# Making the third weight piece of the one-hot rows on GpSimd in a graph network kernel (Trainium2)

## The chip, the cores and the metric

The kernel runs on one core of one Trainium2 chip. The metric is the device time of one execution in microseconds (us). A core has TensorE (PE, with its weight loads shown as PEld), VectorE (DVE), ScalarE (ACT), GpSimd (POOL) and SyncE (SP), each with an instruction queue of its own; the engines synchronise by semaphores. Tiles lie in on-chip memory (SBUF) or in the accumulator memory of TensorE (PSUM).

## The reference

Four graph layers run one after the other on 6250 nodes of 64 features and 206250 edges sorted by destination. Two of them end in a weighted sum over edges, and these two are what the change touches:

```
# second network: attention weights a = exp(e - max) / sum over the edges of a destination
out = segment_sum(a[:, None] * nfeat[src], dst, num_segments=6250)
# fourth network: given edge weights
messages = x[src] * edge_weights[:, None]
out = segment_sum(messages, tgt, num_segments=6250)
```

## The kernel before, in words

A weighted sum (`weighted_sum(n)`, n = 0 for the attention weights and n = 1 for the edge weights) does no gather of rows. The edges are held in blocks of 128 record slots by 64 positions, two blocks to a "pair", 37 pairs (`NDB`) to a sum. For each pair the kernel builds the matrix A[source node, slot] that holds the weight of each edge at its source, and then multiplies it with the node features X. A source node is written as two digits, a low one of 128 values (`P`) and a high one of 49 (`NB`). A is the product of two one-hot tables, built column by column on TensorE.

A pair takes 8 steps (`HS`) of 16 columns (`HC`), and a step takes 2 units of 8 columns (`UC`); so a pair is 16 units and each sum has 296 steps. The tables of a step lie in a ring of 2 (`ring = t % 2`).

- **VectorE, `onehots_of_step` (L1441 to L1461).** L1453 waits for the pair's codes and weights (`cw`), L1455 waits until TensorE has used up the ring's previous contents (`wgt_psum` of the step two earlier). Then three instructions: L1456 makes the high digit's one-hot rows `ohhi` (784 bf16 elements per partition) and signals `hi_made`; L1457 makes the low digit's rows `ohlo` (2048 elements) and signals `codes_ready`; L1461 multiplies `ohhi` by the weight. The float32 weight is split in three bf16 pieces, so that L1461 writes three tables, `ohw`, of 784 elements each (2352), and signals `hot_ready`. Every input and output of the three is in SBUF. In two of the eight steps of a pair VectorE also does small work: L1474 (two adds of a finished window into `acc`) and L1483 (two tables `spot`).
- **TensorE, `products_of_unit` (L932 to L961).** For n = 0 alone: L947, 16 matmuls of `ohlo` by `ohhi`, the adjacency counts. For both sums: it waits for `hot_ready` (L951, on even units) and for ScalarE (L953), then L959 does 48 matmuls, of 8 columns, 3 weight pieces and 2 halves. In 13 of a pair's 16 units (`MIXED`) `pair` (L963) adds L987: 4 of the 49 products X by A of the pair before, which are 8 matmul records in the profile. L995 and L977 fold and place the result once a pair. TensorE's program of a sum is not a hardware loop but is written out in full (L1002).
- **ScalarE, `pair` (L697).** L709 casts the adjacency of a unit to uint8 (n = 0 alone), L714 copies a unit of A from PSUM; each 128 x 784.
- **SyncE, `pair` (L513).** For n = 0 it stores the adjacency (L520). It waits for `hot_ready` of a pair's last step (L522) and loads the pair after next into `cw` (L525).
- **GpSimd (L574 to L636).** Index gathers and scatters by DMA in the earlier stages; its last gather (L615, reached through `gather_chunks`) is over before sum 0 begins. During both sums it runs nothing; between them it writes one row of ones (L636), after a wait for the end of sum 0.

All orders are written out by hand, with a semaphore behind each step.

Of the kernel before, what the change touches and what calls it, by code (L numbers as in the profile page):

```python
# [26 lines left out]
ALU = mybir.AluOpType  # L27
# [3 lines left out]
P = 128  # L31
# [3 lines left out]
NB = -(-N // P)  # L35
# [24 lines left out]
NDB = NRB // 2  # L60
UC = 8
GU = KC // UC
HC = 2 * UC
HS = P // HC
# [27 lines left out]
def gnn(nc, x_in, src, dst, etype, eweight, conv_W, conv_b, att_W, conv_nw, conv_nb, hid_W, hid_b, hid_nw, hid_nb,  # L92
        head_w, head_b, tail_w, tail_b, rel_w, W1_root, W1_rel, b1, W2_root, W2_rel, b2, out):
    with ExitStack() as ctx:
# [3 lines left out]
        def sem(name):  # L98
            return ctx.enter_context(nc.semaphore(name))
# [115 lines left out]
        cw = space[:, at:at + 5 * P].bitcast(BF16).rearrange("p (h x) -> p h x", h=2); at += 5 * P  # L215
# [94 lines left out]
        half_moved = sem("half_moved"); weight_rows = [sem(f"weight_rows{q}") for q in range(NWT)]; wt_psum = sem("wt_psum"); wt_split = sem("wt_split")  # L310
        wt_masked = sem("wt_masked"); denom_ready = sem("denom_ready"); denom_moved = sem("denom_moved"); denom_put = sem("denom_put")
        w_kept = sem("w_kept"); codes_stored = sem("codes_stored"); w_stored = sem("w_stored"); w_split = sem("w_split"); w_first = sem("w_first"); w_rest = sem("w_rest"); cw_loaded = [sem("cw_loaded0"), sem("cw_loaded1")]
        hi_made = sem("hi_made"); codes_ready = sem("codes_ready"); hot_ready = sem("hot_ready")
        adj_psum = sem("adj_psum"); adj_made = sem("adj_made"); wgt_psum = sem("wgt_psum"); wgt_made = sem("wgt_made")
        mixed = sem("mixed"); rowt_ready = sem("rowt_ready"); slot_rows = sem("slot_rows"); slots_copied = sem("slots_copied")
        spot_ready = sem("spot_ready"); spotted = sem("spotted"); summed = sem("summed"); half_summed = sem("half_summed")
# [18 lines left out]
        def _(sp):  # L335
# [177 lines left out]
            def pair(n, i, h, more=True):  # L513

                if n == 0:
                    for b in range(2):
                        sp.wait_ge(adj_made, i * (4 * GU) + (2 * h + b + 1) * GU)
                        sp.sem_inc(sp_ok, 1)
                        at = slice(4 * i + 2 * h + b, 4 * i + 2 * h + b + 1) if isinstance(i, int) else bass.ds(i * 4 + (2 * h + b), 1)
                        sp.dma_start(adj_d[at].rearrange("b p x -> (b p) x"), adj[:, b, :, :].rearrange("p a s -> p (a s)")).then_inc(adj_stored[b], 16)  # L520
                if more:
                    sp.wait_ge(hot_ready, i * (2 * HS) + (n * NDB * HS + (h + 1) * HS))  # L522
                    sp.sem_inc(sp_ok, 1)
                    at = slice(2 * i + h + 2, 2 * i + h + 3) if isinstance(i, int) else bass.ds(i * 2 + (h + 2), 1)
                    sp.dma_start(cw[:, h, :], cw_d[n, at].rearrange("d p x -> (d p) x")).then_inc(cw_loaded[h], 16)  # L525
# [48 lines left out]
        def _(pool):  # L574
# [37 lines left out]
            def gather_chunks(out, table, each):  # L612

                for b in range(NRB):
                    nc.gpsimd.indirect_dma_start(out=out[:, b * each:(b + 1) * each], out_offset=None, in_=table,  # L615
                                                 in_offset=bass.IndirectOffsetOnAxis(ap=half_rec[:, b:b + 1], axis=0)).then_inc(
                                                     rec_rows if table is rec_d else weight_rows[b // 8], 16)
# [12 lines left out]
            pool.wait_ge(wt_psum, NWT)  # L630
            pool.wait_ge(scan_stored, 16 * (LAYERS + 1))
            gather_chunks(wrow, scans_d.rearrange("(c e) a -> c (e a)", e=KC), KC)
            for h in range(2):
                pool.wait_ge(adj_stored[h], 16 * NDB)
            pool.wait_ge(summed, NDB)
            nc.gpsimd.memset(xT[F:F + 1, :], 1.0).then_inc(ones_back, 1)  # L636


        @block.scalar
# [132 lines left out]
        def _(pe):  # L772
# [159 lines left out]
            def products_of_unit(n, i, h, k):  # L932

                u = i * (4 * GU) + (n * NDB * 2 * GU + h * 2 * GU + k + 1)
                hot = i * (2 * HS) + (n * NDB * HS + h * HS + k // 2 + 1)
                early = k if isinstance(i, int) and n + i + h == 0 else 2
                ring = (k // 2) % 2
                if n == 0:
                    if k % 2 == 0:
                        pe.wait_ge(codes_ready, hot)  # L940
                    if early >= 1:
                        pe.wait_ge(adj_made, u - 1)
                    for c in range(UC):
                        col = (k % 2) * UC + c
                        for w in range(2):
                            lo, hi = KC * w, KC * w + KC
                            mm = nc.tensor.matmul(psum[:, w, c * NB:(c + 1) * NB], ohlo[lo:hi, ring, col // 2, :, col % 2],  # L947
                                                  ohhi[lo:hi, ring, col // 2, :, col % 2], start=True, stop=True)
                    mm.then_inc(adj_psum, 1)
                if k % 2 == 0:  # L950
                    pe.wait_ge(hot_ready, hot)  # L951
                if early >= 2:
                    pe.wait_ge(wgt_made, u - 2)  # L953
                for c in range(UC):
                    col = (k % 2) * UC + c
                    for r in range(3):
                        for w in range(2):
                            lo, hi = KC * w, KC * w + KC
                            mm = nc.tensor.matmul(psum[:, 2 + 2 * (k % 2) + w, c * NB:(c + 1) * NB], ohlo[lo:hi, ring, col // 2, :, col % 2],  # L959
                                                  ohw[lo:hi, ring, r, col // 2, :, col % 2], start=(r == 0), stop=(r == 2))  # L960
                mm.then_inc(wgt_psum, 1)  # L961
# [104 lines left out]
        def _(dve):  # L1066
# [374 lines left out]
            def onehots_of_step(n, i, h, t):  # L1441

                done = i * (2 * HS) + (n * NDB * HS + h * HS + t)
                ring = t % 2

                def pairs_of(v, wide):
                    return v.rearrange("p (s e) -> p s e", e=2).unsqueeze(2).to_broadcast([P, UC, wide, 2])

                def table(wide):
                    return digits[:, 0:wide, :].unsqueeze(1).to_broadcast([P, UC, wide, 2])  # L1450

                if t == 0:
                    dve.wait_ge(cw_loaded[h], i * 16 + 16 * (n * (NDB // 2 + 1 - h) + 1))  # L1453
                if not (isinstance(i, int) and n + i + h == 0 and t < 2):
                    dve.wait_ge(wgt_psum, i * (4 * GU) + 2 * (n * NDB * HS + h * HS + t - 1))  # L1455
                nc.vector.tensor_tensor(ohhi[:, ring, :, :, :], pairs_of(cw[:, h, P + t * HC:P + (t + 1) * HC], NB), table(NB), ALU.is_equal).then_inc(hi_made, 1)  # L1456
                nc.vector.tensor_tensor(ohlo[:, ring, :, :, :], pairs_of(cw[:, h, t * HC:(t + 1) * HC], P), table(P), ALU.is_equal).then_inc(codes_ready, 1)  # L1457
                dve.wait_ge(hi_made, done + 1)
                three = cw[:, h, 2 * P + t * 3 * HC:2 * P + (t + 1) * 3 * HC].rearrange("p (k s e) -> p k s e", k=3, e=2).unsqueeze(3).to_broadcast([P, 3, UC, NB, 2])
                each = ohhi[:, ring, :, :, :].unsqueeze(1).to_broadcast([P, 3, UC, NB, 2])  # L1460
                nc.vector.tensor_tensor(ohw[:, ring, :, :, :, :], each, three, ALU.mult).then_inc(hot_ready, 1)  # L1461

            def pair(n, i, h, bases, unit=True, mix=True, put=True):

# [156 lines left out]
```

## Time and profile before

| | us |
|---|---|
| median of 3 runs | 5945.24 (5943.95 to 5957.6) |
| the profiled execution, its own time | 5958.42 |
| its span in the profile | 5956.6 |
| sum 0: first to last start of L1456 | 2673.8 to 3997.8 |
| sum 1: first to last start of L1456 | 4918.7 to 5901.1 |
| PE, DVE, ACT, POOL busy | 3969.0, 3499.9, 2094.0, 736.3 |

Times are us from the span's start. A row of grouped instructions reads: line, engine, operation, output<-input, shapes, count | busy us, mean ns of one | idle us of the engine before them and what ended it. "x8" in a row of the timeline means that neighbouring instructions were merged.

### The profile page before, as it was taken

The page shows a single profiled execution, that of the slowest core. Times are in us where ns is not written, and L with a number is a line of the kernel's source. Part 1 is how long each engine was busy: PE and PEld are TensorE (multiplying, and loading weights), DVE is VectorE, ACT ScalarE, POOL GpSimd, SP SyncE. Part 2 cuts the span into 40 slices and gives each one's busy share as a digit, 9 for nine tenths or more (in the row PEclk, how much of TensorE's full clock was granted, in tenths as well). Part 3 has the DMA queues.
Part 4 walks back from the last instruction along what each step waited for, and adds up shares of the span by engine and source line. Part 5 has one row for each costly group of instructions (what it writes and reads, how often), then busy time and mean ns, then how long its engine had stood idle before and what let it go on. Part 6 is the DMA issues. An engine that isn't in the chain of part 4 may idle for free.

```text
span 5956.6 us, 236270 instructions
## 1 busy us (share of the span) xinstructions
PE 3969.0 (67%) x108221; PEld 3202.8 (54%) x108221; DVE 3499.9 (59%) x4015; ACT 2094.0 (35%) x2443; POOL 736.3 (12%) x758
## 2 busy tenths in 40 slices
PE   0015514804724813818888888887999988999997
PEld 0005513803723812806666666666988976666665
DVE  4532711731571741847676666666535539999997
ACT  4100000011001010007676676664635624555453
POOL 0033263072133033040000000000000000000000
PEclk9996755955865955959999999998989978999998
DMA  6722400520420501511111111114525510000000
GB/s 173 235 64 68 123 17 8 165 63 4 141 74 1 172 6 32 169 49 52 52 57 51 52 58 51 52 49 135 178 100 168 178 65 10 10 11 11 10 11 16
DMA packets 229352, 437.54 MB, mean 73 GB/s; under 512 B 115490, under 2 KB 139940, under 8 KB 228628
## 3 DMA queue, kind: packets, MB, share of 16 engines
q1 hardware_dynamic: 204784, 416.14, 22.1%
q0 software_dynamic: 23904, 10.76, 0.9%
q8 instruction: 635, 10.40, 0.7%
q14 instruction: 29, 0.24, 0.0%
HBM read 317.98 MB, written 112.84 MB: 72 GB/s over the span
## 4 chain that ended last, share of the span: by engine, by line
PE 62%; issue 15%; DVE 12%; ACT 3%; DMA 2%; another core or an unknown queue 2%; POOL 2%; SPq 2%; DVEq 0%; ACTq 0%; POOLq 0%
PE psum L987 16%; PE psum L959 12%; PE psum L836 12%; PE psum L1017 10%; PE psum L947 3%; PE psum L867 2%; PE psum L823 2%; DMA space<-digit_rows 2%; ACT space L709 1%; DVE space L1461 1%; PE psum L869 1%; DVE space L1143 1%; PE psum L1026 1%; PE psum L816 1%
## 5 line engine op out<-in xcount | busy, mean ns | idle before, releaser
L714 ACT COPY space<-psum 128x784 f32<-128x784 f32 x1184 | 966.2, 816 | 631.1 <-PE psum L959 629.0
L959 PE MATMUL psum<-space 64*128 64x49 bf16 x56832 | 990.4, 185 | 181.5 <-issue 152.3
L959 PEld LDWEIGHTS psum<-space 64*128 64x128 bf16 x56832 | 855.7, 95 | 391.2 <-issue 282.9
L987 PE MATMUL psum<-space,X 128*64 128x256 f32 x7252 | 1041.1, 398 | 13.6 <-issue 11.1
L836 PE MATMUL psum<-table,space 128*128 128x56 bf16 x24300 | 701.9, 189 | 347.8 <-issue 333.8
L836 PEld LDWEIGHTS psum<-table,space 128*128 128x128 fp8e4 x24300 | 671.3, 96 | 378.2 <-issue 367.2
L1268 DVE TENSOR_REDUCE space<-psum 128x1512 f32 x300 | 520.0, 1733 | 531.0 <-remote 379.0
L1461 DVE TENSOR_TENSOR space<-space 128x2352 bf16<-128x2352 bf16 x592 | 815.0, 1377 | 0.0
L1457 DVE TENSOR_TENSOR space<-space,V 128x2048 bf16<-128x2048 bf16 x592 | 721.5, 1219 | 0.0
L1017 PE MATMUL psum<-space 128*128 128x192 bf16 x7252 | 628.4, 247 | 23.9 <-DVE space L1536 23.9
L709 ACT CAST space<-psum 128x784 uint8<-128x784 f32 x592 | 482.9, 816 | 400.7 <-PE psum L947 398.1
L1017 PEld LDWEIGHTS psum<-space 128*128 128x128 bf16 x7252 | 594.9, 98 | 49.7 <-issue 48.9
L1456 DVE TENSOR_TENSOR space<-space,V 128x784 bf16<-128x784 bf16 x592 | 335.3, 566 | 460.9 <-PE psum L959 443.5
L987 PEld LDWEIGHTS psum<-space,X 128*64 128x64 f32 x7252 | 467.9, 138 | 197.4 <-issue 36.7
L816 PE MATMUL psum<-ident,X 128*64 128x128 f32 x539 | 104.5, 356 | 646.6 <-DVE X L1236 296.3
L751 ACT CAST space<-space 128x3200 bf16<-128x3200 uint8 x148 | 422.9, 2858 | 258.8 <-PE psum L1017 252.7
L1536 DVE CAST space<-space 128x3072 bf16<-128x3072 uint8 x148 | 260.5, 1760 | 307.2 <-PE psum L1017 304.9
L816 PEld LDWEIGHTS psum<-ident,X 128*64 128x64 f32 x539 | 64.1, 139 | 687.0 <-issue 317.0
L680 ACT ACTIVATE space<-space 128x1620 f32<-128x1620 f32 x4 | 6.2, 1552 | 985.9 <-DVE space L1377 985.9
L601 POOL DMA_INDIRECT heads_d<-spread,heads_at x280 | 261.3, 933 | 596.6 <-DVE spread L1255 512.9
L947 PEld LDWEIGHTS psum<-space 64*128 64x128 bf16 x9472 | 173.0, 95 | 261.9 <-issue 238.9
L609 POOL DMA_INDIRECT gath<-scans_d,ends x196 | 206.6, 1054 | 749.0 <-DMA scans_d<-space 690.5
(277 smaller groups left out, 2785.8 us busy)
## 6 DMA issues: line engine op xcount, KB each, us to landing
space<-onehots SPq DMA_DIRECT2D x300, 432.0 KB
space<-adj_d SPq DMA_DIRECT2D x148, 784.0 KB, 4.3
adj_d<-space SPq DMA_DIRECT2D x74, 784.0 KB, 3.6
onehots<-space SPq DMA_DIRECT2D x60, 432.0 KB, 2.9
space<-digit_rows SPq DMA_DIRECT2D x60, 378.0 KB
space<-cw_d SPq DMA_DIRECT2D x74, 160.0 KB, 3.3
cw_d<-space SPq DMA_DIRECT2D x4, 1184.0 KB
heads_d<-spread,heads_at POOLq DMA_INDIRECT x280
```

Of the source, the lines that this page charges most:

```text
L709: nc.scalar.copy(adj[:, b, :, :].rearrange("p a (w s) -> p w a s", w=2)[:, :, :, c:c + UC], psum[:, 0:2, 0:UC * NB].rearrange("p w (s a) - ...
L714: nc.scalar.copy(A[:, h, :, b * P:(b + 1) * P].rearrange("p a (w s) -> p w a s", w=2)[:, :, :, c:c + UC], psum[:, 2 + 2 * (k % 2):4 + 2 * ...
L751: nc.scalar.copy(adjb[:, r % 2, 0:HALF], adj8[:, r % 2, 0:HALF]).then_inc(cast_act, 1)
L836: mm = nc.tensor.matmul(pb[(h % 2) * NBK + b][:, t * HI:(t + 1) * HI], ohr[:, h, c:c + P].bitcast(FP8), table[:, r, :], start=(r == 0), st ...
L947: mm = nc.tensor.matmul(psum[:, w, c * NB:(c + 1) * NB], ohlo[lo:hi, ring, col // 2, :, col % 2], ohhi[lo:hi, ring, col // 2, :, col % 2], ...
L959: mm = nc.tensor.matmul(psum[:, 2 + 2 * (k % 2) + w, c * NB:(c + 1) * NB], ohlo[lo:hi, ring, col // 2, :, col % 2], ohw[lo:hi, ring, r, co ...
L987: mm = nc.tensor.matmul(pb[6][half:half + F, 0:2 * P], X[:, a, :], A[:, 1 - h, a, :], start=(a < 2), stop=(a >= NB - 2))
L1017: mm = nc.tensor.matmul(pb[r % 2][:, 0:3 * F].rearrange("p (k f) -> p k f", k=3), adjb[:, r % 2, a * P:(a + 1) * P], pieces[:, :, a * F:(a ...
L1268: nc.vector.tensor_reduce(peF[:, bass.ds(t, CH)].rearrange("p (b t) -> p b t", t=PB), banks, AX, ALU.max).then_inc(pick_read, 1)
L1456: nc.vector.tensor_tensor(ohhi[:, ring, :, :, :], pairs_of(cw[:, h, P + t * HC:P + (t + 1) * HC], NB), table(NB), ALU.is_equal).then_inc(h ...
L1457: nc.vector.tensor_tensor(ohlo[:, ring, :, :, :], pairs_of(cw[:, h, t * HC:(t + 1) * HC], P), table(P), ALU.is_equal).then_inc(codes_ready, 1)
L1461: nc.vector.tensor_tensor(ohw[:, ring, :, :, :, :], each, three, ALU.mult).then_inc(hot_ready, 1)
```

## The change

The third of the three products of L1461 moves to GpSimd. VectorE's instruction covers pieces 0 and 1 (1568 elements), and a GpSimd multiply covers piece 2 (784 elements) and signals a new semaphore `third_ready`. GpSimd waits for `hi_made` of the step. TensorE (at L951) and SyncE (at L522) each wait for `third_ready` in addition to `hot_ready`. GpSimd runs the 296 steps of sum 0 behind its last gather and ahead of the wait for the end of sum 0, and the 296 steps of sum 1 behind the row of ones.

```diff
@@ SyncE, pair
                     sp.wait_ge(hot_ready, i * (2 * HS) + (n * NDB * HS + (h + 1) * HS))
+                    sp.wait_ge(third_ready, i * (2 * HS) + (n * NDB * HS + (h + 1) * HS))
                     sp.sem_inc(sp_ok, 1)
@@ GpSimd
             gather_chunks(wrow, scans_d.rearrange("(c e) a -> c (e a)", e=KC), KC)
+            def third_of_step(n, i, h, t):
+
+                ring = t % 2
+                pool.wait_ge(hi_made, i * (2 * HS) + (n * NDB * HS + h * HS + t + 1))
+                third = cw[:, h, 2 * P + t * 3 * HC + 2 * HC:2 * P + (t + 1) * 3 * HC].rearrange("p (s e) -> p s e", e=2).unsqueeze(2).to_broadcast([P, UC, NB, 2])
+                nc.gpsimd.tensor_tensor(ohw[:, ring, 2, :, :, :], ohhi[:, ring, :, :, :], third, ALU.mult).then_inc(third_ready, 1)
+
+            def thirds_of_weights(n):
+
+                for h in range(2):
+                    for t in range(HS):
+                        third_of_step(n, 0, h, t)
+                with pool.Fori(1, NDB // 2) as i:
+                    for h in range(2):
+                        for t in range(HS):
+                            third_of_step(n, i, h, t)
+                for t in range(HS):
+                    third_of_step(n, NDB // 2, 0, t)
+
+            thirds_of_weights(0)
             for h in range(2):
                 pool.wait_ge(adj_stored[h], 16 * NDB)
             pool.wait_ge(summed, NDB)
             nc.gpsimd.memset(xT[F:F + 1, :], 1.0).then_inc(ones_back, 1)
+            thirds_of_weights(1)
@@ TensorE, products_of_unit
                     pe.wait_ge(hot_ready, hot)
+                    pe.wait_ge(third_ready, hot)
@@ VectorE, onehots_of_step
-                three = cw[:, h, 2 * P + t * 3 * HC:2 * P + (t + 1) * 3 * HC].rearrange("p (k s e) -> p k s e", k=3, e=2).unsqueeze(3).to_broadcast([P, 3, UC, NB, 2])
-                each = ohhi[:, ring, :, :, :].unsqueeze(1).to_broadcast([P, 3, UC, NB, 2])
-                nc.vector.tensor_tensor(ohw[:, ring, :, :, :, :], each, three, ALU.mult).then_inc(hot_ready, 1)
+                two = cw[:, h, 2 * P + t * 3 * HC:2 * P + t * 3 * HC + 2 * HC].rearrange("p (k s e) -> p k s e", k=2, e=2).unsqueeze(3).to_broadcast([P, 2, UC, NB, 2])
+                each = ohhi[:, ring, :, :, :].unsqueeze(1).to_broadcast([P, 2, UC, NB, 2])
+                nc.vector.tensor_tensor(ohw[:, ring, 0:2, :, :, :], each, two, ALU.mult).then_inc(hot_ready, 1)
```

## Rows read from the trace of the kernel before

**Rows 1.** Busy time by stretch: most of sum 0, then most of sum 1.

```profile
core 0: us, PE busy (x) PEld busy (x) DVE busy (x) ACT busy (x) POOL busy (x), PEclk, DMA share, GB/s
2750.00:3987.00 1237.00, 1073.49 (x38786) 771.33 (x38786) 853.64 (x961) 864.78 (x1200) 0.00 (x0) 0.97 0.14 53
5000.00:5880.00 880.00, 848.48 (x28842) 597.94 (x28842) 813.88 (x925) 440.25 (x594) 0.00 (x0) 1.00 0.04 10
```

**Rows 2.** L1456 alone, sum 0 and then sum 1: first and last start.

```profile
L1456 DVE TENSOR_TENSOR space<-space,V x296: 559/568/570, 2673.8 to 3997.8; 128x784 bf16<-128x784 bf16 x148
...
  PE psum L959: 383.1, 291
```

```profile
L1456 DVE TENSOR_TENSOR space<-space,V x296: 556/567/570, 4918.7 to 5901.1; 128x784 bf16<-128x784 bf16 x148
...
  PE psum L959: 60.4, 124
```

**Rows 3.** The waits of sum 1 from 5000 to 5880: us in total, times, longest.

```profile
DVE space L1456 <- PE psum L959: 53.2, 113, 0.5
PEld psum L959 <- DVE space L1461: 25.7, 65, 0.6
PE psum L959 <- DVE space L1461: 17.2, 33, 0.5
```

**Rows 4.** Busy time of one whole pair of sum 1.

```profile
5303.46:5330.00 26.54, 25.63 (x876) 18.07 (x878) 24.66 (x28) 13.34 (x18) 0.00 (x0) 1.00 0.04 10
```

**Rows 5.** The page's groups: the three table instructions, both sums.

```profile
L1461 DVE TENSOR_TENSOR space<-space 128x2352 bf16<-128x2352 bf16 x592 | 815.0, 1377 | 0.0
L1457 DVE TENSOR_TENSOR space<-space,V 128x2048 bf16<-128x2048 bf16 x592 | 721.5, 1219 | 0.0
...
L1456 DVE TENSOR_TENSOR space<-space,V 128x784 bf16<-128x784 bf16 x592 | 335.3, 566 | 460.9 <-PE psum L959 443.5
```

**Rows 6.** Timeline of VectorE in sum 1, a step without a wait for TensorE.

```profile
5318.60 1.38 DVE L1461 TENSOR_TENSOR space<-space 128x2352 bf16<-128x2352 bf16 x1
5319.89 0.56 DVE L1456 TENSOR_TENSOR space<-space,V 128x784 bf16<-128x784 bf16 x1
5320.37 1.22 DVE L1457 TENSOR_TENSOR space<-space,V 128x2048 bf16<-128x2048 bf16 x1
5321.50 1.38 DVE L1461 TENSOR_TENSOR space<-space 128x2352 bf16<-128x2352 bf16 x1
```

**Rows 7.** Groups of VectorE in that pair of sum 1: the small work.

```profile
L1474 DVE TENSOR_TENSOR space<-psum,space 64x128 f32 x2 | 0.6, 279 | 0.1
L1483 DVE TENSOR_SCALAR V<-iota_row,slot_rel 128x128 f32<-128x128 f32 x2 | 0.5, 282 | 0.0
```

**Rows 8.** What GpSimd runs in the whole span, apart from other DMAs.

```profile
L636 POOL MEMSET space<- 1x6288 f32 x1 | 5.3, 5334 | 1374.0 <-DVE space L1474 1374.0
L575 POOL IOTA iota_row<- 128x128 f32 x1 | 0.2, 228 | 0.4 <-POOLq L1611 0.4
...
L577 POOL IOTA iota_col<- 128x1 f32 x1 | 0.1, 127 | 0.0
L1611 POOL MEMSET const-bfloat16-1.0<- 128x1 bf16 x1 | 0.1, 106 | 0.0
```

**Rows 9.** Timeline of GpSimd: the gap between two of its instructions.

```profile
2301.36 0.95 POOL L601 DMA_INDIRECT heads_d<-spread,heads_at  x1 [0.30 <-issue]
```

**Rows 10.** Busy time where sum 1 starts, with no L987 in it yet.

```profile
4934.00:4943.00 9.00, 6.83 (x312) 6.42 (x307) 9.00 (x10) 4.88 (x6) 0.00 (x0) 0.50 0.02 4
```

**Rows 11.** Timeline of TensorE: at the lower clock, then at full clock.

```profile
4939.23 2.18 PE L959 MATMUL psum<-space 64*128 64x49 bf16 x96 [0.72 <-DVE space L1461]
```

```profile
3323.11 1.97 PE L987 MATMUL psum<-space,X 128*64 128x256 f32 x8
...
3325.01 0.52 PE L947 MATMUL psum<-space 64*128 64x49 bf16 x16
```

```profile
5303.34 1.08 PE L987 MATMUL psum<-space,X 128*64 128x256 f32 x8
```

More of the change, by code:

```diff
@@ L312, in gnn @@
         w_kept = sem("w_kept"); codes_stored = sem("codes_stored"); w_stored = sem("w_stored"); w_split = sem("w_split"); w_first = sem("w_first"); w_rest = sem("w_rest"); cw_loaded = [sem("cw_loaded0"), sem("cw_loaded1")]
-        hi_made = sem("hi_made"); codes_ready = sem("codes_ready"); hot_ready = sem("hot_ready")
+        hi_made = sem("hi_made"); third_ready = sem("third_ready"); codes_ready = sem("codes_ready"); hot_ready = sem("hot_ready")
         adj_psum = sem("adj_psum"); adj_made = sem("adj_made"); wgt_psum = sem("wgt_psum"); wgt_made = sem("wgt_made")
```

## The prediction

> **What bounds the kernel now.** I began with the busy shares by stretch. In most of sum 0 [rows 1] TensorE is busy 1073.49 of 1237 us (87%), VectorE 853.64 (69%) and ScalarE 864.78 (70%); in most of sum 1 TensorE is busy 848.48 of 880 (96%) and VectorE 813.88 (92%). GpSimd does nothing in either. So in sum 0 TensorE leads and VectorE waits; in sum 1 the two run almost level.
>
> Next the pace. L1456 starts once a step; 295 intervals from first to last start [rows 2] give (3997.8 - 2673.8) / 295 = 4.49 us a step in sum 0, 35.9 us a pair, and (5901.1 - 4918.7) / 295 = 3.33 us a step in sum 1, 26.6 us a pair. Before L1456 VectorE idles for TensorE's L959 for 383.1 us in sum 0, but only 60.4 us in sum 1.
>
> Then the waits of sum 1 [rows 3]. They go both ways: VectorE waits 53.2 us for TensorE's L959, and TensorE waits 17.2 us (its weight loads 25.7) for VectorE's L1461. The pair of 26.54 us [rows 4] shows what is to be had at most: TensorE is busy 25.63 us of it, so taking VectorE away altogether gives 0.91 us a pair.
>
> **What leaves VectorE.** The three table instructions take 566, 1219 and 1377 ns for 784, 2048 and 2352 elements [rows 5]. From 2048 to 2352 that is 158 / 304 = 0.52 ns an element, and 784 elements less make L1461 1377 - 407 = 970 ns. The cost per element is the same line through all three shapes, so I expect no other rate for 1568 elements. Unblocked, a step of VectorE runs from one L1461 to the next in 5321.50 - 5318.60 = 2.90 us [rows 6]; it becomes 2.49. With the small work, 2 x 0.28 + 2 x 0.28 us, taken at 1.1 a pair [rows 7], VectorE needs 8 x 2.90 + 1.1 = 24.3 us a pair now and 21.0 afterwards, if nothing else touches it.
>
> **What GpSimd gets.** 296 multiplies in each sum, of 784 bf16 elements with two inputs. The trace has no GpSimd arithmetic at all. Nearest are a memset of 6288 elements in 5334 ns, 0.85 ns an element, and iotas with (228 - 127) / 127 = 0.80; a one-element memset is 106 ns [rows 8]. One pass at the memset's rate is 784 x 0.85 + 0.1 = 0.77 us: the lower bound. Two reads and a write, each a pass of its own, are 3 x 0.67 + 0.1 = 2.1 us: the upper bound. I take 1.8 us, because this instruction has all three streams where the memset has one, so it is nearer the upper end. Between GpSimd instructions 0.30 us pass [rows 9]; I keep 0.3 a step for handing over.
>
> The Trainium skill (GPSIMD Engine Reference, section 3.1) gives about 2.6 cycles of 1.2 GHz for an element of a two-input op, which would be an estimate of 1.7 us here; no row shows it, and the sum by it would be some 40 us lower.
>
> **Do the two run side by side?** That is what decides. Rows show nothing against it and nothing for it: there is no stretch in which GpSimd reads tiles while VectorE works. So both ends must be priced. If they overlap freely, 1.8 + 0.3 us of GpSimd fit in a step of 3.33 us, and its cost is nil (the cover is VectorE's own 1219 + 970 ns behind `hi_made`, about as long). If GpSimd and VectorE exclude each other while reading SBUF, the multiply is added to VectorE's time: a step is 2.49 + 1.8 + 0.3 = 4.6 us. VectorE has no instruction in a step that isn't a two-input read of SBUF, so GpSimd could hide only in VectorE's idle time. I take the second.
>
> The Trainium skill speaks for the second (SBUF — State Buffer, section "Who interferes with whom"): a VectorE instruction with two SBUF inputs and a GpSimd instruction that reads SBUF exclude each other, and whichever comes later stands still until the first has ended. No row shows this; by the rule the time is the serial one, without it that of the first rival.
>
> **The sum.** A pair takes VectorE and GpSimd together 8 x 4.6 + 1.1 = 37.9 us. Who wins a handover doesn't matter: if VectorE always goes first it runs at most two steps ahead (the ring), must then wait for TensorE, and GpSimd catches up in that wait. Sum 1: 37.9 - 26.6 = 11.3 us a pair, times 37 = +418 us. Sum 0: 37.9 - 35.9 = 2.0, times 37 = +74 us. In sum 0 TensorE is also idle 13% of its pair [rows 1], 4.8 us, much of it ended by nothing that a row names; when VectorE leads, such a pause is partly absorbed by the ring and partly added. I take half of it, 2.4 x 37 = +89 us. Together +581 us.
>
> **Edits at nothing.** TensorE's added wait costs its issue only; behind it are L959 and all else of TensorE, which is why a late third is a late step, counted above. SyncE's added wait delays L525 by one multiply at a pair's end, while these codes are due a pair later (26 us or more); the adjacency store queued behind it comes due four steps later. GpSimd's queue holds nothing else during the sums, its last gather ends before them, and the row of ones waits for the end of sum 0 anyway.
>
> The profiled execution took 5958.42 us, 13 above the median of 5945.24. The increments belong to one execution and are laid on the median: 5945 + 581 = 6526 us, **my forecast (chance 0.62)**. Its own range, from multiplies of 1.5 to 2.1 us and all or none of the pauses, is 6330 to 6730: 0.3 us a step is 8 x 0.3 x 74 = 178 us, and the pauses 89 up or down.
>
> **Rivals.**
> 1. *Free overlap, faster (0.12).* VectorE has 21.0 us of work a pair and TensorE 25.6, so TensorE leads throughout sum 1. It decides if a multiply beside VectorE's reads lengthens neither and stays below some 3 us. Gain: 0.91 x 37 = 34 us, and 8 x 0.41 = 3 us in the first pair, which has no L987 and follows VectorE [rows 10]; nothing in sum 0, where VectorE waits already. Time 5908. For it: the free cycles of GpSimd and the 17.2 us of waits in rows 3. Against: the gain's ceiling is low.
> 2. *Overlap that pays for itself (0.04).* The two-engine slowdown just fills VectorE's 3.3 us of a pair: 5930 to 5960.
> 3. *Short or partial exclusion (0.10).* With 0.77 us the step is 3.56 us and the pair 29.6: 3.0 x 37 = +111 in sum 1, none in sum 0, 6056. Up to 1.5 us, some 6330.
> 4. *TensorE's clock falls too (0.12).* Where sum 1 starts, with TensorE idle 0.72 us before each 96 matmuls [rows 11], the granted clock is 0.50, which is the 1.2 GHz level [rows 10]. In the new kernel TensorE would have 3.5 us of work in 4.6, gaps of about 1.1 us a step. At that level a unit's L959 takes 2.18 / 2 = 1.09 us, L987 1.97 us against 1.08, L947 0.52 us [rows 11]. A pair of sum 1 is then 16 x 1.09 + 12.25 x 1.97 + 2 = 43.6 us, above the 37.9 of VectorE, and one of sum 0 8.3 more, 51.9. All the time at it: (43.6 - 26.6 + 51.9 - 35.9) x 37 = 1221 us, 7166. But so paced TensorE has no gaps and the clock should return, so half of what lies above the serial sum: 6526 + 320 = 6846.
>
> That the change doesn't do what it says is the case where VectorE's two-piece instruction keeps its 1.38 us; with exclusion that adds 0.41 x 8 x 74 = 243 us. I see no reason for it.
>
> **Numbers.** Faster by over 0.3% 0.12; within 0.3% (about what a measurement of this kernel can tell from no change) 0.04; slower 0.84. The range runs from the short multiply's 6060 to 6900, just over the half of rival 4: it holds the forecast, nearly all of 3 and some 0.7 of 4, about 0.80.
>
> **What would show it.** Right: L1461's successor at 0.97 us alone; VectorE's or GpSimd's recorded durations stretched, or idle before VectorE's instructions that ends with GpSimd; L1456's pace near 4.6 us in sum 1; TensorE waiting for GpSimd or VectorE in most steps. Wrong: L1456 to L1461 unchanged in length beside a GpSimd multiply, and a pace of 3.2 us in sum 1. A granted clock under 0.9 in the sums speaks for rival 4; a multiply recorded at 0.8 us for rival 3.

## The result, and the profile after

The changed kernel takes 6167.85 us (median of 4 runs, 6163.02 to 6175.68) against 5944.59 us (4 runs of the kernel before on the same chip): a ratio of 1.0373, 95% interval 1.0352 to 1.0394. It is slower, as forecast, but by 223 us and not by the 581 of the forecast. The profiled execution has a span of 6170.8 us (before: 5956.6). Below, a table instruction is named by its line in the changed kernel: L1479, L1480 and L1484 on VectorE are the former L1456, L1457 and L1461, L982 and L1010 on TensorE the former L959 and L987; L639 is GpSimd's multiply.

The page's groups, which answer to [rows 5]:

```profile
L639 POOL TENSOR_TENSOR space<-space 128x784 bf16<-128x784 bf16 x592 | 1498.8, 2533 | 1953.2 <-DVE space L1479 1953.2
...
L1484 DVE TENSOR_TENSOR space<-space 128x1568 bf16<-128x1568 bf16 x592 | 1254.5, 2119 | 0.0
...
L1480 DVE TENSOR_TENSOR space<-space,V 128x2048 bf16<-128x2048 bf16 x592 | 719.0, 1214 | 0.0
...
L1479 DVE TENSOR_TENSOR space<-space,V 128x784 bf16<-128x784 bf16 x592 | 349.2, 590 | 264.6 <-PE psum L982 251.3
```

The instruction that lost a third of its elements went from 1377 to 2119 ns. Its mean hides two kinds; the line's own view gives them (duration min/median/max):

```profile
L1484 DVE TENSOR_TENSOR space<-space x592: 956/2267/2275, 2660.1 to 6109.4; 128x1568 bf16<-128x1568 bf16 x198
```

0.96 us is what 1568 elements cost (forecast: 0.97), 2.27 us is that and 1.31 us more. In the timeline, 289 of the 296 in sum 0 and 236 of the 296 in sum 1 are of the long kind.

Where the time went is seen from the pace of L1479, as in [rows 2]; here first sum 0, then sum 1:

```profile
L1479 DVE TENSOR_TENSOR space<-space,V x296: 550/567/569, 2658.5 to 3984.5; 128x784 bf16<-128x784 bf16 x148
...
  PE psum L982: 151.6, 134
...
L1479 DVE TENSOR_TENSOR space<-space,V x296: 546/553/1579, 4902.7 to 6107.8; 128x784 bf16<-128x784 bf16 x148
...
  PE psum L982: 99.8, 75
```

Sum 0 lasts 3984.5 - 2658.5 = 1326.0 us, before it was 1324.0: nothing. What VectorE lost came out of its wait for TensorE, which fell from 383.1 to 151.6 us. Sum 1 lasts 6107.8 - 4902.7 = 1205.1 us, before it was 982.4: +222.7, the whole loss. (The two profiled spans differ by 214.2 us: the stages ahead of sum 0 were 15 us shorter in this execution, and the end behind sum 1 is 7.5 us longer.) A pair takes 32.7 us there in place of 26.6.

The timeline of VectorE and GpSimd in sum 1 shows the usual pattern:

```profile
5515.22 0.55 DVE L1479 TENSOR_TENSOR space<-space,V 128x784 bf16<-128x784 bf16 x1
5515.69 1.21 DVE L1480 TENSOR_TENSOR space<-space,V 128x2048 bf16<-128x2048 bf16 x1
5515.85 2.41 POOL L639 TENSOR_TENSOR space<-space 128x784 bf16<-128x784 bf16 x1 [1.78 <-DVE space L1479]
5516.83 2.27 DVE L1484 TENSOR_TENSOR space<-space 128x1568 bf16<-128x1568 bf16 x1
5519.02 0.55 DVE L1479 TENSOR_TENSOR space<-space,V 128x784 bf16<-128x784 bf16 x1
```

A step is 5519.02 - 5515.22 = 3.80 us, which is the forecast's 2.49 and 1.31. There is no gap in it: the stretched instruction is where VectorE stands still. The multiply is recorded from 0.16 us after L1480's start for 2.41 us, 0.9 us longer than the 1.50 us that it takes when it gets its turn at once (18 of the 296 in sum 1). So up to L1480's end it stands still too.

In 60 steps of sum 1 L1484 is short: 42 multiplies are passed over. Such a multiply asks during L1480, doesn't get its turn when L1480 ends, and waits until VectorE stops for TensorE. For 24 of them that is right behind L1484 of the same step, after 0.9 us. For the other 18 VectorE first runs a second step, whose own multiply queues behind the overdue one:

```profile
5903.74 0.55 DVE L1479 TENSOR_TENSOR space<-space,V 128x784 bf16<-128x784 bf16 x1
5904.22 1.21 DVE L1480 TENSOR_TENSOR space<-space,V 128x2048 bf16<-128x2048 bf16 x1
...
5904.38 7.25 POOL L639 TENSOR_TENSOR space<-space 128x784 bf16<-128x784 bf16 x2 [1.78 <-DVE space L1479]
...
5905.36 0.96 DVE L1484 TENSOR_TENSOR space<-space 128x1568 bf16<-128x1568 bf16 x1
...
5906.24 0.55 DVE L1479 TENSOR_TENSOR space<-space,V 128x784 bf16<-128x784 bf16 x1
5906.72 1.21 DVE L1480 TENSOR_TENSOR space<-space,V 128x2048 bf16<-128x2048 bf16 x1
5907.85 0.96 DVE L1484 TENSOR_TENSOR space<-space 128x1568 bf16<-128x1568 bf16 x1
5910.24 1.08 PEld L982 LDWEIGHTS psum<-space 64*128 64x128 bf16 x48 [3.65 <-issue]
...
5913.65 0.57 DVE L1479 TENSOR_TENSOR space<-space,V 128x784 bf16<-128x784 bf16 x1 [4.84 <-PE psum L982]
```

VectorE runs two steps in full, at their unblocked lengths. Only when the ring stops it at 5908.8 do the two multiplies run. TensorE's weight loads meanwhile idle 3.65 us, its matmuls 3.2 (the view says "issue", but what it needs is the third piece), and VectorE then waits 4.84 us for TensorE. There are 18 such stalls on the 37 pairs of sum 1; 17 of them end in a wait of L1479 of 3.6 to 5.5 us, 73.8 us in all of the 99.8 for which VectorE idles before L1479.

Every one of the 42 multiplies belongs to the step right behind VectorE's small work of the pair, L1497 (24) or L1506 (18), where L1479 follows that work without a gap; no other step's multiply is the first to be passed over. Why a small instruction ahead of the step has this effect, no run here shows.

The granted clock is 0.88 in sum 1, where it was 1.00. Behind a stall it is 0.50, the 1.2 GHz level; the second row is the part of the 4.84 us in which TensorE works again:

```profile
5000.00:6000.00 1000.00, 868.53 (x26641) 605.59 (x26642) 914.17 (x855) 408.50 (x549) 640.58 (x245) 0.88 0.03 8
5910.24:5913.65 3.41, 3.38 (x110) 2.59 (x112) 0.00 (x0) 0.81 (x1) 1.39 (x1) 0.50 0.16 48
```

### The profile page after: what moved, and what is told of

Its sections match the earlier page's. It is cut to its first block, busy times and chain, and to the rows that moved or that the text cites. A ratio compares the mean times of both kernels' runs of the same rounds, so it can differ in the third digit from the quotient of the medians.

```text
span 6170.8 us, 237478 instructions
## 1 busy us (share of the span) xinstructions
PE 4071.7 (66%) x108221; PEld 3268.0 (53%) x108221; DVE 3936.5 (64%) x4015; ACT 2096.0 (34%) x2443; POOL 2239.6 (36%) x1350
## 4 chain that ended last, share of the span: by engine, by line
PE 53%; issue 18%; DVE 18%; POOL 3%; DMA 2%; another core or an unknown queue 2%; ACT 2%; SPq 1%; DVEq 1%; ACTq 0%; POOLq 0%
PE psum L1010 11%; PE psum L858 11%; PE psum L1040 10%; PE psum L982 9%; DVE space L1484 5%; PE psum L969 3%; PE psum L889 2%; POOL gath L610 2%; PE psum L845 2%; DMA space<-digit_rows 2%; DVE space L1479 2%; PE psum L891 1%; DVE space L1166 1%; DVE space L1480 1%
## 5 line engine op out<-in xcount | busy, mean ns | idle before, releaser
L639 POOL TENSOR_TENSOR space<-space 128x784 bf16<-128x784 bf16 x592 | 1498.8, 2533 | 1953.2 <-DVE space L1479 1953.2
L1484 DVE TENSOR_TENSOR space<-space 128x1568 bf16<-128x1568 bf16 x592 | 1254.5, 2119 | 0.0
L982 PE MATMUL psum<-space 64*128 64x49 bf16 x56832 | 1026.9, 188 | 321.8 <-issue 178.0
L982 PEld LDWEIGHTS psum<-space 64*128 64x128 bf16 x56832 | 894.6, 97 | 556.7 <-issue 328.2
L1010 PE MATMUL psum<-space,X 128*64 128x256 f32 x7252 | 1087.5, 413 | 12.8 <-issue 10.4
L1480 DVE TENSOR_TENSOR space<-space,V 128x2048 bf16<-128x2048 bf16 x592 | 719.0, 1214 | 0.0
L1010 PEld LDWEIGHTS psum<-space,X 128*64 128x64 f32 x7252 | 481.7, 143 | 208.5 <-issue 52.6
L1479 DVE TENSOR_TENSOR space<-space,V 128x784 bf16<-128x784 bf16 x592 | 349.2, 590 | 264.6 <-PE psum L982 251.3
```

What stands on the lines that cost most here:

```text
L639: nc.gpsimd.tensor_tensor(ohw[:, ring, 2, :, :, :], ohhi[:, ring, :, :, :], third, ALU.mult).then_inc(third_ready, 1)
L1010: mm = nc.tensor.matmul(pb[6][half:half + F, 0:2 * P], X[:, a, :], A[:, 1 - h, a, :], start=(a < 2), stop=(a >= NB - 2))
L1484: nc.vector.tensor_tensor(ohw[:, ring, 0:2, :, :, :], each, two, ALU.mult).then_inc(hot_ready, 1)
```

## The experiments

The theory: **exclusion**. While GpSimd reads SBUF, VectorE's instruction stands still, and the other way round. Rivals: **traffic** (any GpSimd instruction, or the added signals, slow VectorE), **lateness** (VectorE is only a symptom; TensorE waits for a slow third piece) and **clock** (the loss is TensorE's lower clock). Diffs are against the changed kernel unless said otherwise. In each experiment the time that follows "against", and the ratio, are from the kernel before on the same chip.

### In which sum

In `sum0_only` GpSimd makes the third piece in sum 0 alone; in sum 1 VectorE writes all three, and TensorE and SyncE wait for `hot_ready` alone. Part of the edit:

```diff
-                    pe.wait_ge(third_ready, hot)
+                    if n == 0:
+                        pe.wait_ge(third_ready, hot)
...
-            thirds_of_weights(1)
```

`sum1_only` is the same with `n == 1`, and `third_ready` is raised by the count of sum 0 ahead of sum 1.

> GpSimd makes the third piece in sum 0 alone; in sum 1 VectorE makes all three as before. If VectorE's slack in sum 0 covers the exclusion (in the changed kernel its wait for TensorE fell from 383 to 152 us and sum 0 kept its 4.49 us a step): as before, 5945, within 10 us. If both sums pay something and the pace of sum 0 was a coincidence: 5960 to 6050.

Measured: 5955.52 against 5951.33 us, ratio 1.001 (0.9994 to 1.0025). Sum 0 takes 1323.3 us although 288 of its 296 two-piece instructions are 2.27 us long.

> GpSimd makes the third piece in sum 1 alone. If the whole loss lies in sum 1: as the changed kernel, 6168 within 10 us, with L1484's instruction at 2.27 us in four steps of five. If some of it lies in sum 0: 6100 or less.

Measured: 6168.17 against 5951.33 us, ratio 1.0356 (1.0324 to 1.0388); sum 1 takes 1200.8 us, with 252 long instructions. So the loss is sum 1's. Sum 0 pays with VectorE's idle time, and TensorE goes on at its own pace.

### The ceiling

```diff
                     sp.wait_ge(hot_ready, i * (2 * HS) + (n * NDB * HS + (h + 1) * HS))
-                    sp.wait_ge(third_ready, i * (2 * HS) + (n * NDB * HS + (h + 1) * HS))
...
                     pe.wait_ge(hot_ready, hot)
-                    pe.wait_ge(third_ready, hot)
...
-            thirds_of_weights(0)
...
-            thirds_of_weights(1)
...
                 link(nc.vector.memset(acc, 0.0))
+                link(nc.vector.memset(ohw[:, 0, 2, :, :, :], 0.0))
+                link(nc.vector.memset(ohw[:, 1, 2, :, :, :], 0.0))
```

> VectorE makes two pieces, GpSimd nothing, and nobody waits for it; the third table is set to zero once a sum, so a third of the weights' multiplication is left out. This is the ceiling of the change. VectorE needs 21.0 us a pair, TensorE 25.6: 5908 (the sum of my first rival), 5900 to 5915. If VectorE counted for more in sum 0 than its wait shows, lower than 5890.

Measured: 5946.42 against 5951.33 us, ratio 0.999 (0.9974 to 1.0006): no difference, where I expected 37 us. The interval leaves room for at most 0.3%. Sum 1 takes 976.7 us in place of 982.4. VectorE does have less to do, but its wait for TensorE rises from 60 to 176 us. The timeline of this kernel at a pair's end shows why (L1477, L1478, L1482 are the three table instructions, L978 is TensorE's product):

```profile
5302.05 0.57 DVE L1477 TENSOR_TENSOR space<-space,V 128x784 bf16<-128x784 bf16 x1 [0.46 <-PE psum L978]
...
5303.19 0.66 PE L1014 MATMUL psum<-fold,V 128*128 128x64 f32 x4 [0.47 <-ACT V L745]
...
5305.95 0.40 PE L978 MATMUL psum<-space 64*128 64x49 bf16 x17 [0.68 <-issue]
```

At a pair's end TensorE still waits, 0.47 us for ScalarE's copy and 0.68 us inside L978, and VectorE waits as well. Neither engine alone ends such a pair. Over 5000 to 5880 us TensorE is busy 850.91 us, before 848.48 [rows 1], so nearly all of its idle time stayed: the 0.91 us of it in [rows 4] was not VectorE's to give back.

### Does GpSimd have to read?

```diff
-                with pool.Fori(1, NDB // 2) as i:
+                for i in range(1, NDB // 2):
...
-                nc.gpsimd.tensor_tensor(ohw[:, ring, 2, :, :, :], ohhi[:, ring, :, :, :], third, ALU.mult).then_inc(third_ready, 1)
+                nc.gpsimd.memset(ohw[:, ring, 2, :, :, :], 0.0).then_inc(third_ready, 1)
```

> As the changed kernel with all its signals, but GpSimd writes zeros in place of multiplying: it reads nothing (the third product is left out). Exclusion by GpSimd's reads alone: VectorE's two-piece instruction at 0.96 us in every step and the time of the kernel without the third piece, near 5910. If any GpSimd instruction, or the added signals and waits themselves, do the harm: 2.27 us again and above 6050. If VectorE is slowed only in proportion to GpSimd's traffic: in between.

Measured: 5946.63 against 5951.33 us, ratio 0.9984 (0.9969 to 1.0), the ceiling again. Its timeline:

```profile
5400.85 1.22 DVE L1480 TENSOR_TENSOR space<-space,V 128x2048 bf16<-128x2048 bf16 x1
5400.99 0.75 POOL L639 MEMSET space<- 128x784 bf16 x1 [3.16 <-DVE space L1479]
5401.98 0.97 DVE L1484 TENSOR_TENSOR space<-space 128x1568 bf16<-128x1568 bf16 x1
```

GpSimd writes its 784 elements wholly inside L1480, and neither is longer for it; all 592 of L1484 take 0.96 us. The signals, the waits and GpSimd's writes cost nothing. **Traffic** falls. (GpSimd's loop is written out in this kernel; that isn't the cause, for in `pool_one_input` below it is written out too, and there L1484 is stretched.)

### How long is VectorE shut out?

Half the elements (the first half of the third piece is left out and set to zero once a sum):

```diff
-                nc.gpsimd.tensor_tensor(ohw[:, ring, 2, :, :, :], ohhi[:, ring, :, :, :], third, ALU.mult).then_inc(third_ready, 1)
+                nc.gpsimd.tensor_tensor(ohw[:, ring, 2, UC // 2:, :, :], ohhi[:, ring, UC // 2:, :, :], third[:, UC // 2:, :, :], ALU.mult).then_inc(third_ready, 1)
```

> GpSimd multiplies only the second half of the third piece, 392 elements with two inputs (the first half is left out and stays zero). Exclusion for the instruction's length, of some 0.1 us and the rest in proportion: 0.1 + 0.6 = 0.7 us, so VectorE's two-piece instruction at 1.65 us, step 3.15 us, 5910 to 5950. A fixed cost of handing over would leave it near 2.27 us and 6168.

Measured: 5987.35 against 5969.32 us, ratio 1.0028 (1.0013 to 1.0042); sum 1 1006.3 us.

```profile
5400.00 1.76 POOL L639 TENSOR_TENSOR space<-space 128x392 bf16<-128x392 bf16 x1 [1.39 <-DVE space L1481]
5400.98 1.61 DVE L1486 TENSOR_TENSOR space<-space 128x1568 bf16<-128x1568 bf16 x1
```

1.61 - 0.96 = 0.65 us for 392 elements, 1.31 for 784: in proportion, 1.67 ns an element, and next to nothing fixed. The time is 18 us above that of the kernel before. It is above the 5950 I had allowed, in part because the kernel before takes 5969 us on this chip. And I had overlooked this: with the small work VectorE needs 8 x 3.14 + 1.1 = 26.2 us a pair, a little more than TensorE's 25.6, and where the two run level each still waits for the other now and then (VectorE idles 51.5 us for TensorE in sum 1).

One input in place of two:

```diff
-                nc.gpsimd.tensor_tensor(ohw[:, ring, 2, :, :, :], ohhi[:, ring, :, :, :], third, ALU.mult).then_inc(third_ready, 1)
+                nc.gpsimd.tensor_scalar(ohw[:, ring, 2, :, :, :], ohhi[:, ring, :, :, :], 0.0, None, ALU.mult).then_inc(third_ready, 1)
```

> GpSimd multiplies the high digit's rows by the constant 0, so it reads one tile in place of two (the weights are left out of the third piece). If an instruction that reads at all shuts VectorE out for its own length, and one read costs about half of two: VectorE's two-piece instruction at 0.96 + 0.7 = 1.7 us, a step of 3.2 us, sum 1 led by TensorE again: 5910 to 5960. If only two-input GpSimd instructions exclude: 0.96 us and 5910. If the length of exclusion is a fixed 1.31 us whatever is read: 2.27 us and 6168.

Measured: 6018.37 against 5969.32 us, ratio 1.0076 (1.0047 to 1.0104), outside what I gave.

```profile
5404.27 0.57 DVE L1479 TENSOR_TENSOR space<-space,V 128x784 bf16<-128x784 bf16 x1
5404.75 1.22 DVE L1480 TENSOR_TENSOR space<-space,V 128x2048 bf16<-128x2048 bf16 x1
5405.89 1.61 DVE L1484 TENSOR_TENSOR space<-space 128x1568 bf16<-128x1568 bf16 x1
```

VectorE loses 0.65 us, half of 1.31, as one read in place of two would make it. But GpSimd's instruction is recorded longer:

```profile
L639 POOL TENSOR_SCALAR space<-space x592: 3076/3080/3083, 2667.5 to 5965.2; 128x784 bf16<-128x784 bf16 x198
```

Each of its 592 instructions is recorded at 3.08 us, where the two-input multiply beside the same L1480 has 2.41. About 1.06 us of it lie ahead of L1480's end; whether it stands still in them, as the two-input multiply does, no run shows, so its length alone is between 2.0 and 3.08 us. Either way, being busy and shutting VectorE out are two things: of the 2.0 us behind L1480's end only 0.65 hurt L1484. The rest of the loss here (1033.9 us for sum 1) is argued and not shown by a run of its own. The third piece comes 3.2 us after `hi_made`, about as late as a step is long, and TensorE's waits for VectorE's L1484, which in part end with the third piece, are 55.4 us between 5000 and 5880 in place of 17.2 [rows 3]: a small case of **lateness**. And the small one-input L1506 is longer too, 0.53 or 0.66 us in place of 0.27.

Twice the multiply:

```diff
+        spare = space[:, at:at + HC * NB].bitcast(BF16).rearrange("p (r s a e) -> p r s a e", r=2, a=NB, e=2); at += HC * NB
...
+                nc.gpsimd.tensor_tensor(spare[:, ring, :, :, :], ohhi[:, ring, :, :, :], third, ALU.mult)
                 nc.gpsimd.tensor_tensor(ohw[:, ring, 2, :, :, :], ohhi[:, ring, :, :, :], third, ALU.mult).then_inc(third_ready, 1)
```

> GpSimd multiplies twice in a row, first into a spare tile and then the piece itself. Exclusion: each multiply takes 1.31 to 1.44 us of VectorE's time, so a step is 2.49 + 2.7 = 5.2 us, 42.7 us a pair: sum 1 +10 us a pair = +370, sum 0 (35.9) +6.8 a pair = +250: 6750 to 6850, both sums led by VectorE and GpSimd together. If the loss came from TensorE's wait for a late third alone: the third comes 1.4 us later and VectorE's instruction keeps 2.27 us, 6300 to 6500.

Measured: 6694.64 against 5969.32 us, ratio 1.1224 (1.119 to 1.1258), 55 us under the range that I gave for exclusion and far above the one for lateness. The timeline (L1481, L1482, L1486 are the table instructions, L640 and L641 the multiplies):

```profile
5512.48 1.21 DVE L1482 TENSOR_TENSOR space<-space,V 128x2048 bf16<-128x2048 bf16 x1
5512.63 2.41 POOL L640 TENSOR_TENSOR space<-space 128x784 bf16<-128x784 bf16 x1 [0.50 <-DVE space L1481]
5513.61 2.26 DVE L1486 TENSOR_TENSOR space<-space 128x1568 bf16<-128x1568 bf16 x1
5515.01 2.22 POOL L641 TENSOR_TENSOR space<-space 128x784 bf16<-128x784 bf16 x1
5515.80 1.85 DVE L1481 TENSOR_TENSOR space<-space,V 128x784 bf16<-128x784 bf16 x1
5517.57 1.21 DVE L1482 TENSOR_TENSOR space<-space,V 128x2048 bf16<-128x2048 bf16 x1
```

The first multiply stretches L1486 by 1.31 us, the second, let in after it, L1481 from 0.57 to 1.85. A step is 5517.57 - 5512.48 = 5.09 us, 2.49 + 2 x 1.31 = 5.11. The sums now take 1518.6 and 1514.8 us, since sum 0's slack is used up. That is the serial sum of the prediction with the right term in it. **Lateness**, which would leave VectorE's instructions at their own lengths, is not what rules here.

### Does VectorE need two inputs to be shut out?

```diff
-                nc.vector.tensor_tensor(ohw[:, ring, 0:2, :, :, :], each, two, ALU.mult).then_inc(hot_ready, 1)
+                nc.vector.tensor_scalar(ohw[:, ring, 0:2, :, :, :], each, 0.5, None, ALU.mult).then_inc(hot_ready, 1)
```

> VectorE's two-piece instruction multiplies the rows by a constant, so it reads one tile in place of two (the first two pieces lack their weights). GpSimd's multiply stays. If only VectorE instructions with two inputs from SBUF are shut out: this one runs at its own length (0.9 us or less) beside GpSimd's multiply, GpSimd's is recorded near 2.4 us, and the time is 5900 to 5960. If any VectorE instruction is shut out (the small one-input L1506 was stretched from 0.48 to 1.7 us in the kernel with two multiplies): near 2.2 us again and 6100 to 6170.

Measured: 5478.81 against 5391.17 us, ratio 1.0164 (1.0147 to 1.018). This chip runs the stages ahead of the sums in some 550 us less; the sums themselves take what they took elsewhere (see the last section), so differences and ratios are to be read, not the times. The loss is 88 us, between the two cases that I gave (none, or 150 and more): the instruction is shut out, but alone it is so short that a step is only 2.49 - 0.96 + 1.86 = 3.39 us.

```profile
4808.50 1.22 DVE L1480 TENSOR_TENSOR space<-space,V 128x2048 bf16<-128x2048 bf16 x1
4808.66 2.41 POOL L639 TENSOR_TENSOR space<-space 128x784 bf16<-128x784 bf16 x1 [1.07 <-DVE space L1479]
4809.64 1.86 DVE L1484 TENSOR_SCALAR space<-space 128x1568 bf16<-128x1568 bf16 x1
```

```profile
L1484 DVE TENSOR_SCALAR space<-space x592: 549/1861/1868, 2124.0 to 5429.7; 128x1568 bf16<-128x1568 bf16 x198
```

Alone this instruction takes 0.55 us (the minimum), beside the multiply 1.86: 1.31 again. A one-input instruction of this kind is shut out in full. The Trainium skill (SBUF — State Buffer, section "Who interferes with whom") has it so for `tensor_scalar` in its two-port modes; that 0.55 us for 1568 elements, against 0.96 for the two-input form, is such a mode is my reading, not a thing that the trace names.

### Who goes first

GpSimd asks later, after VectorE's two pieces:

```diff
-                pool.wait_ge(hi_made, i * (2 * HS) + (n * NDB * HS + h * HS + t + 1))
+                pool.wait_ge(hot_ready, i * (2 * HS) + (n * NDB * HS + h * HS + t + 1))
```

> GpSimd waits for VectorE's two pieces in place of the high digit's rows, so its multiply is asked for 2.1 us later, when VectorE goes on to the next step's L1479 or waits for TensorE. Exclusion: VectorE's time is the same sum, 2.49 + 1.31 = 3.80 us a step, now with L1479 stretched and L1484 at 0.96 us; but the piece is ready later and GpSimd has to win a handover against the next step's first instructions, so TensorE waits more: 6180 to 6400. If a later start let GpSimd fall into idle time of VectorE: below 6100.

Measured: 5631.61 against 5391.17 us, ratio 1.0449 (1.0432 to 1.0467): 240 us lost, just inside what I gave for exclusion when laid on 5945.

```profile
4804.09 1.50 POOL L639 TENSOR_TENSOR space<-space 128x784 bf16<-128x784 bf16 x1 [2.66 <-DVE space L1484]
4804.11 1.89 DVE L1479 TENSOR_TENSOR space<-space,V 128x784 bf16<-128x784 bf16 x1
4805.93 1.21 DVE L1480 TENSOR_TENSOR space<-space,V 128x2048 bf16<-128x2048 bf16 x1
4807.06 0.96 DVE L1484 TENSOR_TENSOR space<-space 128x1568 bf16<-128x1568 bf16 x1
```

Now L1484 has its 0.96 us and what follows it carries the 1.3 us, mostly the next L1479. The multiply gets its turn at once and is 1.50 us long, in 557 of its 592 cases. Sum 1 takes 1207.7 us, as in the changed kernel: the place of the exclusion moved, the bill didn't.

VectorE waits for the third piece before it starts the next step, so that no multiply is passed over for a second step:

```diff
+                if not (isinstance(i, int) and n + i + h + t == 0):
+                    dve.wait_ge(third_ready, done)
                 nc.vector.tensor_tensor(ohhi[:, ring, :, :, :], pairs_of(cw[:, h, P + t * HC:P + (t + 1) * HC], NB), table(NB), ALU.is_equal).then_inc(hi_made, 1)
```

> VectorE waits for the third piece of the step before it starts the next, so that GpSimd always gets its turn. If the stalls of 4.8 us, 32 in sum 1, in which GpSimd lost two handovers running while TensorE waited for its piece, are what lies above 31.5 us a pair, sum 1 comes to 37 x 31.5 = 1166 us in place of 1205 and the whole to 6130 (6115 to 6145). If they are only a symptom of TensorE's clock or of its own pace, 6168 or more.

Measured: 6173.29 against 5969.32 us, ratio 1.0344 (1.0309 to 1.0378), not separable from the changed kernel's 1.0373. Inside, sum 1 fell from 1205.1 to 1181.1 us, 32.0 a pair, with 11 multiplies passed over in place of 42 and VectorE idle 33 us in place of 100. I had expected 1166 and 6130, from 32 stalls in sum 1 where the timeline has 18. So the stalls are real and worth some 24 us in sum 1. Sum 0 takes 14 us more than in the changed kernel; whether the cure costs that is not shown, for on this chip sum 0 is longer in two kernels without the added wait too (`pool_half` 1336.6 us, `pool_one_input` 1344.3).

Its granted clock in sum 1 is 0.89, hardly above the changed kernel's 0.88:

```profile
5000.00:6000.00 1000.00, 876.65 (x27256) 608.97 (x27249) 967.82 (x873) 418.30 (x560) 607.73 (x249) 0.89 0.03 9
```

At that clock a pair is 32.0 us, and the serial sum without any clock in it is 8 x 3.80 + 1.1 = 31.5. At most 0.5 us a pair, 20 us in all, is left for **clock** and everything else, as long as TensorE's pauses stay short. In the changed kernel the clock is part of the stalls: VectorE waits there while TensorE catches up at 0.50. How the 42 us above the serial sum divide between pause and clock isn't shown.

### Other work on GpSimd

From the kernel before; the two small tables of a pair (L1483 there) move instead:

```diff
-                    if mix and t == 5:
-                        for b in range(2):
...
-                            ins = nc.vector.tensor_scalar(spot[:, 1 - h, b, :], iota_row[:, :], slot_rel[:, block], None, ALU.is_equal)
-                        ins.then_inc(spot_ready, 1)
...
+                if put:
+                    pool.wait_ge(spotted, i * 2 + (n * NDB + h - 1))
+                for b in range(2):
...
+                    ins = nc.gpsimd.tensor_scalar(spot[:, 1 - h, b, :], iota_row[:, :], slot_rel[:, block], None, ALU.is_equal)
+                ins.then_inc(spot_ready, 1)
```

> The kernel before, with VectorE's small one-input work of a pair (L1483, two tables of 128 elements) on GpSimd in place of the third piece: what a better choice of work to move would give. It takes 0.48 us a pair from VectorE and shuts it out for some 0.1 us each. The ceiling measured with the third piece left out was 0.1%, so: no difference, 5935 to 5960 beside 5950. If VectorE's share of the pair's end counts: up to 18 us faster.

Measured: 5396.41 against 5391.17 us, ratio 1.001 (0.9997 to 1.0022): no difference. No version here beats the kernel before; with the ceiling measured at 0.1% (0.3% at the end of its interval), there is next to nothing in this direction.

## Why the prediction was right and wrong

**The sign and the mechanism: right.** GpSimd's multiply and VectorE's instructions run one after the other, and sum 1 pays. The Trainium skill's rule (SBUF — State Buffer, "Who interferes with whom") is what the trace shows, with 1.31 us a step, except that 42 multiplies of sum 1 had asked first and were passed over all the same. `pool_memset` agrees with its other half, that a GpSimd instruction which only writes doesn't contend.

**The size: wrong, by one term of the sum and one addition.** The forecast was 6526 in a range from 6060 to 6900, which holds the measured 6168; but the loss was 223 us where I had 581. The forecast's own range, 6330 to 6730, doesn't hold it; the whole range does because it left room for rival 3, a short exclusion. By its size the result is that rival's, to which I had given 0.10.

- *"I take 1.8 us" and "0.3 a step for handing over".* Together 2.1 us a step were added to VectorE; it was 1.31. The multiply alone is 1.50 us, of which 1.31 shut VectorE out, and there is no handover cost on top: the stretched L1484 follows L1480 as closely as ever, and half the elements cost half the time. I had leant to the bound of three separate passes "because it has all three streams"; `pool_half` shows 1.67 ns an element, two passes at the memset's 0.85. The Trainium skill's figure (GPSIMD Engine Reference, section 3.1) gave an estimate of 1.7 us, a little long as well (it would have lowered the sum by 8 x 0.1 x 74 = 59 us, not by the 40 that I wrote). With 1.31 a step is 3.80 and a pair 31.5 us: sum 1 (31.5 - 26.6) x 37 = +181 in place of +418.
- *"Sum 0: 37.9 - 35.9".* With 31.5 us VectorE stays below TensorE's 35.9, so this term is zero, not 74. `sum0_only` shows it.
- *"I take half of it, 2.4 x 37 = +89 us" for TensorE's pauses in sum 0.* Nothing of the kind was added; VectorE doesn't lead. And where it does, in `pool_twice`, sum 0 takes 1518.6 us and sum 1 1514.8, so TensorE's pauses in sum 0 are absorbed even then.
- *"Who wins a handover doesn't matter."* It does. Of 42 multiplies passed over in sum 1, 18 had to wait for a second step of VectorE as well, and TensorE ran dry. GpSimd does catch up in VectorE's wait, as I wrote, but that wait, of up to 5.5 us, is longer than what the two multiplies would have cost in their turn (2 x 1.31). Sum 1 has 223 us where the serial sum has 181; of these 42 us `turns` takes back 24.
- *Rival 1's gain, 34 and 3 us.* The ceiling is 5 us (`third_left_out`), within the spread of the measurement. I had read TensorE's 0.91 us of idle time in a pair as VectorE's doing. So even free overlap would have made no difference, and its chance of 0.12 should have stood under "same".
- *Rival 4.* The granted clock did fall, to 0.88 in sum 1. Between the stalls it falls on an engine that waits anyway (20 us at most in `turns`); in the stalls it is a part of the 42 us.
- *Bounds.* A multiply of 1.5 us with 0.3 for handing over gives 8 x 4.29 + 1.1 = 35.4 us a pair and 5945 + 326 = 6271, not "some 6330". And the bounds 6330 and 6730 don't hold both terms at once, which would be 6259 and 6793.
- *L1484's 0.97 us*: measured 0.96. *The added waits at nothing*: shown by `pool_memset`.

## What to carry to other kernels

Before moving a piece of VectorE's work to GpSimd, compare the time for which GpSimd reads SBUF (here 1.67 ns an element with two bf16 inputs) with what VectorE saves (0.52 ns an element): where VectorE's neighbours read SBUF too, the move costs three times what it gives, and only VectorE's idle time can pay for it. Measure the ceiling first by leaving the work out; here it was 5 us, so there was nothing to win, however the two engines share. An engine of two that run level is not the bound because the other waits for it now and then.

## What the runs showed of the hardware that I had not expected

- GpSimd's multiply by a constant, with one input, is recorded at 3.08 us for 784 elements where the two-input multiply, asked for at the same point, has 2.41, and yet it shuts VectorE's L1484 out for only 0.65 us in place of 1.31.
- A waiting GpSimd instruction isn't sure of the next turn. In sum 1 of the changed kernel 42 of 296 multiplies were passed over, 18 of them for two steps of VectorE, and all 42 in a step that follows VectorE's small work without a gap. So it is in the other kernels too whose timeline shows it: 7 of 7 in the changed kernel's sum 0, 16 of 16 in `turns`, 31 of 31 in `pool_half`, 37 of 37 in `vector_one_input`.
- A one-input VectorE instruction was stretched by the same 1.31 us, from 0.55 to 1.86.
- Two chips differ by 9% on this kernel (5951 and 5969 us on two of the chips, 5391 on a third), while the sums are alike. In the last experiment, whose stages ahead of the sums are those of the kernel before, sum 0 starts at 2117.1 us, not 2673.8, and then lasts 1323.8; sum 1 lasts 980.7. GpSimd's gather waited 386 us for the stored scans there, against 691 in the kernel before on the other chip; here the row of `spots_on_pool`, then that of the kernel before:

```profile
POOL gath L609 <- DMA scans_d<-space: 385.7, 4, 99.7
```

```profile
POOL gath L609 <- DMA scans_d<-space: 690.5, 4, 173.0
```

What makes these stages longer there stays open.
